# Audio tower, one core: three of eight chunks of the experts' weights split once and loaded as two halves

## The reference, cut to what matters

```python
h = tok(x)                                   # patches -> 256 channels, 8 batches of 376 tokens
h = h + attn(layernorm(h))                   # 16 heads of 64, causal, rope
h = h + moe(layernorm(h))                    # 4 experts, each token goes to 2 of them
h = h + recurrence(layernorm(h))
h = h + quantised_ffn(layernorm(h))

def moe(x):                                  # E = 4, D = 256, F = 1024, all float32
    probs = softmax(x @ router_w + router_b)
    top_p, top_i = top_k(probs, 2)
    gates = zeros.at[token, top_i].add(top_p / sum(top_p))
    hid = silu(einsum('td,edf->etf', x, w1)) * einsum('td,edf->etf', x, w3)
    return einsum('te,etd->td', gates, einsum('etf,efd->etd', hid, w2))
```

## Time and profile before

| | us |
|---|---|
| median of 3 runs | 1753.79 |
| lowest and highest run | 1750.0, 1754.49 |
| the profiled execution, its own time | 1756.17 |
| its span, first to last instruction | 1754.3 |
| mean granted clock of TensorE | 0.924 of full speed |

### The profile page before, as it was taken

The page is one execution under the profiler, slowest core; times in us unless marked ns, Lnnn a source line. Parts: engine busy times, 40 slices in busy tenths (PEclk is TensorE's granted clock), DMA queues, the critical chain, the costliest instruction groups (busy, mean ns, idle before and its releaser), DMA issues. The chain is left out here.

```text
span 1754.3 us, 30236 instructions
## 1 busy us (share of the span) xinstructions
PE 1476.7 (84%) x10725; PEld 1374.2 (78%) x10725; DVE 1223.8 (70%) x2590; ACT 989.0 (56%) x2138; POOL 927.4 (53%) x750
## 2 busy tenths in 40 slices
PE   5389999999999999995699999999988746789039
PEld 4279888888888888885699999999987745788039
DVE  7548677777777777774256666666588489459896
ACT  4547675757575757572455555555543444459552
POOL 4468475858585858572567677776755623000000
PEclk8679999999999999997799999999999968899569
DMA  7490000000000100001665555555544321003313
GB/s 241 147 309 19 19 19 28 28 28 28 28 28 25 31 25 14 25 13 34 193 167 142 138 146 136 148 135 149 140 122 107 66 89 43 11 0 133 110 51 113
DMA packets 86126, 150.38 MB, mean 86 GB/s; under 512 B 7992, under 2 KB 63608, under 8 KB 85720
## 3 DMA queue, kind: packets, MB, share of 16 engines
q1 hardware_dynamic: 75464, 134.62, 24.7%
q0 software_dynamic: 10512, 13.83, 4.6%
HBM read 111.88 MB, written 49.91 MB: 92 GB/s over the span
## 5 line engine op out<-in xcount | busy, mean ns | idle before, releaser
L1589 POOL TENSOR_TENSOR expert_w_low<-expert_raw,expert_w_high 128x768 fp32r<-128x768 f32 x152 | 288.5, 1948 | 172.1 <-ACT expert_w_high L1414 167.0
L855 ACT ACTIVATE expert_raw<-psum,neg_max 120x376 f32<-120x376 f32 (+2 forms) x384 | 176.9, 486 | 106.0 <-DVE neg_max L1041 103.8
L1561 DVE TENSOR_TENSOR expert_act_low<-expert_act,expert_act_high 128x384 fp32r<-128x384 f32 x152 | 140.0, 921 | 79.6 <-ACT expert_act_high L1452 79.0
L1452 ACT ACTIVATE expert_act_high<-expert_act 128x384 fp32r<-128x384 f32 x152 | 79.8, 525 | 204.1 <-DVE expert_act L1556 202.7
L967 POOL TENSOR_TENSOR qk_low<-rotated,qk_high 128x376 fp32r<-128x376 f32 x128 | 127.0, 992 | 95.2 <-ACT qk_high L848 95.2
L1373 PE MATMUL psum<-slots_high,expert_w_high 128*128 128x384 f32 x608 | 161.0, 346 | 16.7 <-DVE expert_act L1556 15.4
L1064 DVE TENSOR_TENSOR pt_low<-psum,pt_high 128x752 fp32r<-128x752 f32 x128 | 120.4, 941 | 69.9 <-ACT pt_high L864 69.5
L1373 PE MATMUL psum<-slots_low,expert_w_high 128*128 128x384 f32 x608 | 157.0, 339 | 0.0
L1373 PE MATMUL psum<-slots_high,expert_w_low 128*128 128x384 f32 x608 | 156.7, 338 | 0.0
L1384 PE MATMUL psum<-expert_w_high,expert_act_high 128*128 128x256 f32 x456 | 134.5, 295 | 11.6 <-ACT slot_out L1434 9.9
L997 POOL TENSOR_TENSOR rotated<-rotated,expert_raw 128x376 f32<-128x376 f32 x128 | 127.7, 998 | 14.5 <-POOL expert_raw L993 0.5
(11 more groups left out here) (305 smaller groups left out, 4380.6 us busy)
## 6 DMA issues: line engine op xcount, KB each, us to landing
expert_raw<-in_experts SPq DMA_DIRECT2D x152, 384.0 KB, 3.1
x_slots<-in_c_slots SPq DMA_DIRECT2D x4, 3168.0 KB, 27.8
slot_rows<-x_slots SPq DMA_DIRECT2D x19, 396.0 KB, 4.5
up_spill<-held SPq DMA_DIRECT2D x5, 1128.0 KB, 5.0
held<-up_spill SPq DMA_DIRECT2D x5, 1128.0 KB, 5.7
attn_x<-tok_xt SPq DMA_DIRECT2D x6, 752.0 KB, 4.0
x_parts<-attn_x SPq DMA_DIRECT2D x6, 752.0 KB, 4.6
patch<-in_patches SPq DMA_DIRECT2D x8, 376.0 KB, 6.8
```

The costliest lines, as they stand in the source:

```text
L855: last = act.activation(probs[0:ni, h % 2, at:at + P * it + ni], score_bank(h % 2, it), ACT.Exp, bias=neg_max[0:ni, h % 2, it:it + 1], acc ...
L1561: dve.tensor_tensor(act_hl[1][:, g % 2, :], act_f[:, g % 2, :], act_hl[0][:, g % 2, :].bitcast(F32), ALU.subtract).then_inc(low_made, 1)
L1589: pool.tensor_tensor(w[1][:, g % RING, :], raw[:, g % RAW, :], w[0][:, g % RING, :].bitcast(F32), ALU.subtract).then_inc(w_low, 1)
```

## The change

Chunks 2, 4 and 6 of every expert are split once, during attention, and both parts are stored to a new tensor in DRAM, `experts_split` (4 experts x 3 chunks x 128 x 2 parts x 768). There are 12 such jobs, two at each of the changes to batches 1 to 6. A job uses the idle `raw`/`swapped` area for the chunk (`whole`) and `pt` for the parts. SyncE waits for the sixth rotation of the coming batch, loads the chunk, waits for both parts and stores them, and does the same for the second job; then come the loads and stores that stood there before. ScalarE makes the high part of both jobs after the values of the first token tile (a wait for the load, and for the stores of the job before), GpSimd the low part after the sixth rotation, ahead of the scatter. ScalarE's first step of the batch waits until both jobs' low parts are made and all stores have landed.

In the experts, SyncE loads both parts of chunks 2, 4 and 6 in one DMA of 768 KB straight into the ring, which is now one tensor `both` with the parts side by side; from tile 1 on it waits for the down product of the chunk eight before. TensorE waits for that load. The splits on ScalarE and GpSimd are left out for these chunks. The other five go on through the four raw buffers, counted by `raw_of`.

```diff
+KEPT_SPLIT = (2, 4, 6)
+KEPT_RAW = tuple(f for f in range(CHUNKS) if f not in KEPT_SPLIT)
+SPLIT_JOBS = [(e, k) for e in range(EXPERTS) for k in range(len(KEPT_SPLIT))]
+SPLIT_BATCHES = range(1, 1 + len(SPLIT_JOBS) // 2)
...
+        whole = shared[:, 0:CHUNK_COLS]
+        parts = [x[:].rearrange("p u k n -> p (u k n)")[:, 0:CHUNK_COLS] for x in pt]
...
+                def load_whole(j):
+                    e, k = SPLIT_JOBS[j]
+                    sp.dma_start(whole, a["experts"][e, KEPT_SPLIT[k], :, :]).then_inc(whole_in, 16)
+
+                def store_parts(j):
+                    e, k = SPLIT_JOBS[j]
+                    sp.wait_ge(parts_low, j + 1)
+                    for part in range(2):
+                        sp.dma_start(split_w[e, k, :, part, :], parts[part].bitcast(F32)).then_inc(parts_stored, 16)
+
                 for b in range(BATCH + 1):
+                    if b in SPLIT_BATCHES:
+                        sp.wait_ge(rot_made, 16 * b + 2 * LEAD + CR_ROT)
+                        load_whole(2 * b - 2)
+                        store_parts(2 * b - 2)
+                        load_whole(2 * b - 1)
+                        store_parts(2 * b - 1)
                     if b:
                         sp.wait_ge(out_kept, T * b)
...
+                def split_part(j):
+                    act.wait_ge(whole_in, 16 * (j + 1))
+                    act.wait_ge(parts_stored, 32 * j)
+                    act.activation(parts[0], whole, ACT.Copy).then_inc(parts_high, 1)
+
                 def begin(b):
                     for at, t in enumerate(VALUE_ORDER):
+                        if at == 1 and b in SPLIT_BATCHES:
+                            split_part(2 * b - 2)
+                            split_part(2 * b - 1)
...
+                    if c == 0 and b in SPLIT_BATCHES:
+                        act.wait_ge(parts_low, 2 * b)
+                        act.wait_ge(parts_stored, 64 * b)
                     turned_high(b, 2 * c)
...
+                def split_part(j):
+                    pool.wait_ge(parts_high, j + 1)
+                    pool.tensor_tensor(parts[1], whole, parts[0].bitcast(F32), ALU.subtract).then_inc(parts_low, 1)
...
+                        if n == 2 * LEAD - 1 and b in SPLIT_BATCHES:
+                            split_part(2 * b - 2)
+                            split_part(2 * b - 1)
                         if b >= 2 and n in SCATTER_AT:
                             scatter(b - 2, SCATTER_AT[n])
...
-        w = [sb(f"expert_w_{part}", [P, RING, CHUNK_COLS], F32R) for part in ("high", "low")]
+        both = sb("expert_w", [P, RING, 2, CHUNK_COLS], F32R)
+        w = [both[:, :, part, :] for part in range(2)]
...
-                        if g >= RAW:
-                            sp.wait_ge(w_low, g - RAW + 1)
-                        if g >= EARLY_CHUNKS:
-                            sp.dma_start(raw[:, g % RAW, :], a["experts"][bass.ds(e, 1), f, :, :]
-                                         .rearrange("e p c -> p (e c)")).then_inc(w_in[g % RAW], 16)
+                        if f in KEPT_SPLIT:
+                            if i:
+                                sp.wait_ge(down_made, g - RING + 1)
+                            k = KEPT_SPLIT.index(f)
+                            sp.dma_start(both[:, f, :, :].bitcast(F32), split_w[bass.ds(e, 1), k, :, :, :]
+                                         .rearrange("e p h c -> p (e h) c")).then_inc(split_in[k], 16)
+                        else:
+                            r = raw_of(g)
+                            if r >= RAW:
+                                sp.wait_ge(w_low, r - RAW + 1)
+                            if r >= EARLY_CHUNKS:
+                                sp.dma_start(raw[:, r % RAW, :], a["experts"][bass.ds(e, 1), f, :, :]
+                                             .rearrange("e p c -> p (e c)")).then_inc(w_in[r % RAW], 16)
...
-                    pe.wait_ge(w_low, g + 1)
+                    if f in KEPT_SPLIT:
+                        pe.wait_ge(split_in[KEPT_SPLIT.index(f)], 16 * (i + 1))
+                    else:
+                        pe.wait_ge(w_low, raw_of(g) + 1)
...
-                    if g + AHEAD < last_chunk:
+                    if g + AHEAD < last_chunk and (g + AHEAD) % CHUNKS in KEPT_RAW:
                         split_high(act, g + AHEAD)
...
-                    if g + AHEAD < last_chunk:
+                    if g + AHEAD < last_chunk and (g + AHEAD) % CHUNKS in KEPT_RAW:
                         split_low(g + AHEAD)
```

More of the change, by code:

```diff
@@ L490, in attention @@
         slots_cleared = sem("slots_cleared")
+        whole_in, parts_high, parts_low, parts_stored = (sem(f"split_w_{n}") for n in ("in", "high", "low", "stored"))
         (summed, std_made, rstd_made, x_made, x_turned, xt_kept, logits_made, odds_read, shifted, odds_made,
@@ L1254, in _, with expert_tiles @@
                 dve.wait_ge(table_made, 1)
-def expert_tiles(nc, psum, a, x_slots, h_rows, onehot, where, raw, w_in, added, ident, vec, first, turn, feed, up_gate, down,
+def expert_tiles(nc, psum, a, x_slots, h_rows, onehot, where, raw, w_in, split_w, added, ident, vec, first, turn, feed, up_gate, down,
                  spent, made):
@@ L1302, in group_dst @@
             return dst if len(dst.shape) == 3 else dst.rearrange("p (k n) -> p k n", k=GROUP)
+        split_in = [sem(f"expert_split_in{k}") for k in range(len(KEPT_SPLIT))]
+        raw_of = lambda g: len(KEPT_RAW) * (g // CHUNKS) + KEPT_RAW.index(g % CHUNKS)
         three = ((0, 0), (0, 1), (1, 0))
@@ L1435, in keep_out @@
                                    scale=gate[:, i % 2, 1:2]).then_inc(y_kept, 1)
-                split_high(act, 0)
-                split_high(act, 1)
-                keep_high(0, 0)
-                keep_high(0, 1)
-                split_high(act, 2)
-                split_high(act, 3)
+                for g in range(AHEAD):
+                    if g == EARLY_CHUNKS:
+                        keep_high(0, 0)
+                        keep_high(0, 1)
+                    if g in KEPT_RAW:
+                        split_high(act, g)
                 for g in range(last_chunk):
@@ L2323, in audio_tower @@
             expert_sems, late_sems = [], []
-            expert_tiles(nc, psum, a, x_slots, h_rows, onehot, where, raw_w, w_in, added, ident, vec, first, turn, feed, up_gate,
+            expert_tiles(nc, psum, a, x_slots, h_rows, onehot, where, raw_w, w_in, split_w, added, ident, vec, first, turn, feed, up_gate,
                          down, front_sems, expert_sems)
```

21 lines of the change are left out of this document (13 added, 8 removed).

## The result

The changed kernel takes 1734.16 us in the median (1733.11 to 1737.82, four runs), the kernel before 1754.14 us beside it (1750.0 to 1755.64, four runs). The ratio is 0.9889, with a 95% interval of 0.987 to 0.9908: 20 us less. The sign and the range of the prediction held, but it forecast 9 us less and 20 came: its 1745 us were 11 us too many.

What follows compares the result with a forecast made beforehand. It took TensorE, busy 84% of the span, as the bound, so gains are only where it stands still in the experts. Experts -33, attention +19, clock +5 gave -9 us: 1745 against the median of 1753.79; range 1725 to 1764.

Steps and rivals of the forecast that it cites:

- the slip: Attention, six changes of batch: the two-job chain takes 18.2 us against 15.0 of room, 3.2 us late each, 19 in all.
- the clock: Attention: TensorE's clock drops after half of the six new stalls, 1.7 us each; 5 us lost, bounds 0 and 10.
- The plateau: Experts, thirteen tiles: fewer splits give back 1.6 of the 1.9 us lost per tile; 21 us gained, bounds 8 and 24.
- my rule that step 6 must lose its split: Experts' tiles: without the second split there, VectorE's 3.53 us low part ends 1.7 us earlier.
- The end of the stage: Experts from 1268 us: eight steps lose the split blocking VectorE's table doublings, 1.6 us each; 12 gained, bounds 7 and 16.
- The loads: Experts: 1.15 MB more per tile, DMA share about 0.75, loads of halves covered by six steps of lead; zero cost.
- The entry: Start of the experts: 0.75 MB more read before up(3), 0 to 2 us lost, taken as 0.
- The rival of late halves: Experts: the 768 KB loads arrive late and TensorE waits for them, 1 us a tile; 1764 us, chance 0.04.
- The rival in which the slip is swallowed: Attention: the chain fits in 16 us and the clock holds, costing 6 us; 1727 us, chance 0.16.
- the one where the chain outweighs the gain: Attention: a slip of 6.4 us plus a clock drop of 1.7 per change, 49 against 33; 1770 us, chance 0.16.

Runs made afterwards that it cites:

- the set 3, 5, 7: The change with two slots for attention's parts and chunks 3, 5 and 7 kept split in place of 2, 4 and 6: 1716.68 us, ratio 0.9788.
- the kernels with jobs alone: Kernel before plus attention's jobs only, experts as before: 1766.87 us with two per change of batch, 1753.72 with one, 1813.87 with three.
- two other kernels with the same jobs: Kernel before plus the twelve attention jobs only, 1766.87 us; the changed kernel with chunks 3, 5 and 7 kept split, one slot, 1732.94 us.
- three jobs a change: Kernel before plus attention's jobs only, three at each of six changes of batch, experts as before: 1813.87 us, ratio 1.0353.
- 2, 4, 6: The change with two slots in attention, the second job's parts beside the first's and its chunk loaded earlier: 1721.68 us, ratio 0.9816.
- 2, 5, 7: The change with two slots for attention's parts and chunks 2, 5 and 7 kept split: 1724.88 us, ratio 0.9843.
- four jobs: The change with chunk 2 alone kept split, one job at each of the changes to batches 1 to 4: 1733.03 us, ratio 0.9887.
- one job: Kernel before plus attention's jobs only, one at each of six changes of batch, experts as before: 1753.72 us, ratio 1.0.

## Why the prediction was right in kind, and what was mis-sized

In the experts it forecast 33 us of gain, and 32.3 came. For attention it put a cost of 24 us, 19 for the slip and 5 for the clock, and 14.4 came. These two terms are what failed.

**The plateau: right.** 21 us from 13 x 1.6, measured 20.9; tiles of 26.3 to 26.8, measured 26.5; L1561 never above some 2 us, measured 1.78. TensorE's own 26.2 us for a tile, worked out from the earlier trace rows, is what the set 3, 5, 7 reaches. The 1.6 of these 1.9 us was a guess that came out well: the stalls that the prediction listed make some 1.0 of it, and no row stood for the other 0.6. The two causes named, the low part behind two splits and the kept output behind ScalarE, were each taken away alone. But my rule that step 6 must lose its split was too narrow. The set 3, 5, 7 leaves it and does better.

**The end of the stage: right.** 12 us from eight blocked pairs, measured 12.5 with eight long instructions fewer. The steps are 3.6 us long (29.0 / 8), forecast 3.5, from 4.2; pairs of 0.36 free and 1.9 beside a split are there. The long stalls mostly went: of three stretches at half the clock before (1277, 1311 and 1345 us, 3.4 us each) one is left, at 1341.

**The loads: right at about zero.** In the experts the 768 KB land after 4.3 us in the median, raw chunks after 5.4 in place of 3.1, and TensorE waits for neither. The DMA share rose to 0.64, not 0.75. The entry lost 1.1 us, within the 0 to 2; as the kernels with jobs alone have entries of 53.8 to 54.2 us and not 55.1, it can be 2. The rival of late halves falls with that.

**Attention: the mechanism right, the size too large.** This is one of the two terms that failed, 19 us where 14 came. The chain was 18.2 us by the sum, in fact 16.6 at batch 2 and 17.3 in the mean of the six. Its pieces at batch 2, in the same order (from the load's issue to the end of the first low part; on to ScalarE's second high part; on to the end of the second low part; the last stores): 5.7, 4.65, 2.8, 3.5 against 5.9, 5.4, 2.8, 4.1. I took the landing of two stores of 384 KB from the transfer of 752 KB into another tensor, 4.1; two stores land 3.4 to 3.7 us after the low part. The load behind them was not the stores plus 1.1, since its issue comes with theirs and its data moves beside them. The rule of the Trainium skill that the prediction set beside the rows ("DMA: Bandwidth & Descriptors", anatomy of one DMA: a fixed 2.0 us and the bytes at 436 GB/s) gave an estimate of 3.8 and a slip of 2.6; measured is 2.3, so its sum was nearer than my row. The section gives this fit for transfers that GpSimd issues, and these are SyncE's. Most of the slip comes through to the end: 14.0 of slips, 14.4 us at the first up product.

**The clock: wrong, 5 us that never came.** It failed in both steps. In the changed kernel it does not fall after the new stalls, of 1.6 us at most (granted 1.00 from 120 to 780 us); in two other kernels with the same jobs it fell once in six changes, behind 1.86 and 2.07 us. And 1.7 us a drop was the wrong price: it is TensorE's own loss in 3.4 us at half speed, and it counts only where TensorE sets the pace. In attention a drop costs nothing, as the 73.28 against 73.29 us show, with the drop in place of a stall, and as three jobs a change show with drops of 6.8 to 10.2 us. That other engines set the pace there fits these rows; no run tests it by itself.

So of the 11 us by which 1745 was too high, 5 are the clock and 5 the slip; the rest is the spread of the runs. The rival in which the slip is swallowed (1727) was right for the clock, but not for the slip. For the one where the chain outweighs the gain it would take the 59 us of three jobs a change.

**What stays open.** The order of merit of the sets: 3, 5, 7 is 5 us better than 2, 4, 6, and 2, 5, 7 is 3 us worse (1.2 us in the stage, 2.1 behind it). The trace shows which links differ (a low part behind GpSimd with 2, 4, 6, ScalarE's kept output with 2, 5, 7, neither with 3, 5, 7). Why 3, 5, 7 has a gap between its two splits, though both are made, was not separated. Nor is it known why two of the kernels have another stretch at half the clock behind the experts. A fourth kept chunk was not tried.

## What to carry to other kernels

In this kernel a VectorE instruction with two operands in SBUF stood behind one of GpSimd's splits for 1.2 us and behind two in a row for 3. Look for VectorE instructions several times as long as their twins, and ask which of GpSimd's neighbours can be made to stand apart; one may be enough (four jobs gave what twelve gave). Try more than one set: which one is best was not foreseen here. When work is moved to a stage with idle engines, compare the length of the serial chain with the room, and not the busy time (one job cost nothing, two 13 us, three 61): write both down, and if the chain is too long, look for a second buffer before giving it up (12.5 us here). Price a drop of TensorE's clock only where TensorE is the bound.

## What the runs showed of the hardware that I had not expected

An instruction of VectorE with two inputs in SBUF (0.56 us alone) behind the first of two back-to-back splits of GpSimd waits for both and takes 3.5 us; with a gap of 0.4 us between the splits it slips in and takes 0.78 (1055.31 above). TensorE at 1.2 GHz for 3.4 us in attention cost under 0.1 us, and 6.8 to 10.2 us of it at each of six stalls of 7.7 to 8.6 us, 2.7 to 5.9 us of it inside the stall, cost nothing either. Two stores of 384 KB issued together landed 3.4 to 3.7 us after the low part before them, and a load issued right behind them was there 3.7 to 4.9 us after its own issue, where the first load of a change took 2.8 to 3.6 (changed kernel).
